# One-hot lanes of every other batch on ScalarE, Gelu's table loaded ahead, and four unread products on TensorE

## The chip, the cores and the metric

The kernel runs on one NeuronCore of a Trainium2 chip. The metric is the device time of one execution in microseconds (us), as the median of several runs. Before the change it is 1257.93 us (three runs, 1257.76 to 1258.65).

## The reference, cut to what matters

One layer of graph attention over 80,000 edges and 2,500 nodes, then a mixture of eight experts of which each node uses two:

```
x = x + relu(segment_sum(alpha * h[src], dst))            # h = layernorm(x) W, 4 heads of 64
xn = layernorm(layernorm(x)) * gamma + beta
logits = xn @ Wr + br;  top_vals, top_idx = top_k(logits, 2);  w = softmax(top_vals)
y = sum over e of  (gelu(xn @ W1[e] + b1[e]) @ W2[e] + b2[e]) * w_full[:, e]
out = x + y
```

Here x is 2500 x 256, W1 is 8 x 256 x 512, W2 is 8 x 512 x 256, everything in float32.

## The kernel before

The program is written by hand, one instruction stream for each engine, tied by semaphores (`wait_ge`, `then_inc`). Each stream is executed in order. It has three stages.

**Edges (to about 950 us).** GpSimd gathers rows of `h` by 664 indirect DMAs (L528). TensorE multiplies them with one-hot matrices of the destination (L640), VectorE weighs and accumulates (L1188, L1101). ScalarE makes those one-hot matrices in float32: for each tile of 128 edges `Square(dst - iota)` (L822), eight tiles at a time, and then `Relu(1 - square)` over the eight (L827), which is 1 where the square is 0, and else 0.

**Routing (950 to 1013 us).** TensorE transposes the nodes and forms the router's logits (L673, L682). VectorE finds each node's two experts and its rank in each, all by short instructions that depend on one another (L1294 to L1363). The result is a position for each of 40 columns of pairs (20 blocks of nodes, twice). A position is split into a lane (its last 7 bits, `lane_i`, copied to bfloat16 as `lane_f`) and a column (`col_f`). To turn the table round, from "where does this pair go" to "which pair sits here", VectorE makes for four batches of ten columns of pairs a one-hot of the lane (`lane_oh`, L1368), a one-hot of the column (`col_eq`, L1370) and its products with the node's lane and with the pair's number (`col_oh`, L1373, L1374). TensorE multiplies the two, 40 products into one PSUM bank (L701). Each batch is given over by `table_in`, the last product gives `table_done`. VectorE then turns the sums into indices (L1389 to L1398), and `where_ready` lets GpSimd start.

**Experts (1013 us to the end).** The pairs, sorted by expert, fill 27 blocks of 256 slots. GpSimd fetches the nodes of a block by two indirect DMAs (L539), four blocks ahead. TensorE runs `slots_T` (four transposes, L715), `layer_1` (eight products of 256 columns, L727) and `layer_2` (eight products, L741), in the order slots_T(0), slots_T(1), layer_1(0), then for each block j layer_1(j+1), slots_T(j+2), layer_2(j). ScalarE applies Gelu (`hidden`, L911), VectorE picks W1 (L1403), scales the transposed nodes (L1411) and adds b2 (L1419), GpSimd scatters the results (L548). At the end the results are read back and combined with the weights (L1460, L1461).

`hidden` is the first place that needs Gelu's table, so ScalarE loads it there. `xn1` holds the normalised nodes, `ones` is a 128 x 128 matrix of ones, `bank[7]` is a PSUM bank that is free between the edges and layer_2 of block 1, `fm` is a 1 x 4 tile of the edges' stage that is no longer read.

Of the kernel before, what the change touches and what calls it, by code (L numbers as in the profile page):

```python
# [37 lines left out]
def gat_moe_kernel(nc, x, src, dst, gnn_w, a_src, a_dst, gamma, beta, wr, br, w1, b1, w2, b2, out):  # L38
    fp32, bf16, i32 = mybir.dt.float32, mybir.dt.bfloat16, mybir.dt.int32
    ALU = mybir.AluOpType  # L40
    ACT = mybir.ActivationFunctionType
    AX = mybir.AxisListType
    P = 128


    N, F = x.shape
    H, _, FO = gnn_w.shape
    HF = H * FO
    KF = F // P
# [22 lines left out]
    assert NT % BT == 0 and CHUNKS * P == E and RING % PH == 0 and H * PH == P  # L72
    MW = HF + H
    NE, _, HID = w1.shape
    FC = HID // P
    BS = 256
# [21 lines left out]
    with ctx:  # L98
        def sb(name, shape, dt=fp32):
            return ctx.enter_context(nc.sbuf_tensor(name, shape, dt))  # L100

        def sem(name):
            return ctx.enter_context(nc.semaphore(name))

        psum = ctx.enter_context(nc.psum_tensor("psum", [P, 8, 512], fp32))
        bank = [psum[:, i, :] for i in range(8)]
# [6 lines left out]
        def early(width, dt=fp32):  # L113

            a = ring_flat[:, used[0]:used[0] + width]
            used[0] += width
            return a if dt == fp32 else a.bitcast(dt)
# [29 lines left out]
        start = early(NB + 1)  # L147
# [31 lines left out]
        ones = sb("ones", [P, P])  # L179
        iota_f = sb("iota_f", [P, P])  # L180
# [21 lines left out]
        old, fm, fm1 = sb("old", [1, H]), sb("fm", [1, H]), sb("fm1", [1, H])  # L202
# [21 lines left out]
        late = early  # L224
        xn1 = late(NB * F).rearrange("p (b f) -> p b f", b=NB)
# [26 lines left out]
        PAIRS = TOP * NB  # L252
        pos_i, lane_i, col_i = (late(PAIRS, i32) for _ in range(3))
        lane_f = late(PAIRS // 2, bf16)
        col_f = late(PAIRS)
        pair_f = late(PAIRS)
        iota_b = late(P // 2, bf16)
        CH = 10
# [6 lines left out]
        def over_x(width):  # L265
# [16 lines left out]
        lane_oh = shared[:, 0:PAIRS * P // 2].bitcast(bf16).rearrange("p (i n) -> p i n", i=PAIRS)  # L282
# [43 lines left out]
        SETS = ((0, 4), (4, 12), (12, NB))  # L326
        assert NB % 2 == 0 and NB % OUT_SET == 0 and SETS[-1][0] < NB - 1
        x_again_in = [sem(f"x_again_in{n}") for n in range(len(SETS))]
        z_stored, table_in, table_done, where_ready = (
            sem(n) for n in ("z_stored", "table_in", "table_done", "where_ready"))  # L330
        xT1_done, xT1_copied, logits_done = (
# [233 lines left out]
        def _(pe):  # L565
# [82 lines left out]
            for n, w in enumerate((wr_g, wr_b)):  # L648
                for k in range(KF):
                    last = pe.matmul(bank[7][:, n * NE:(n + 1) * NE], ones[:, :], w[:, k, :],  # L650
                                     start=(k == 0), stop=(k == KF - 1))
# [3 lines left out]
            for f in range(NPH - 1):  # L655
                n = f * PB
# [10 lines left out]
            def nodes_T(i):  # L667
                pe.wait_ge(x1_made, 1 + sum(2 * i + 2 > hi for _, hi in SETS))
                if i >= 2:
                    pe.wait_ge(xT1_copied, i - 1)  # L670
                for b in range(2):
                    for k in range(KF):
                        last = pe.transpose(bank[i % 2][:, (k * 2 + b) * P:(k * 2 + b + 1) * P],  # L673
                                            acc[:, 2 * i + b, k * P:(k + 1) * P], ident[:, :])
                last.then_inc(xT1_done, 1)
# [22 lines left out]
            for i in range(PAIRS):  # L698
                if i % CH == 0:
                    pe.wait_ge(table_in, i // CH + 1)  # L700
                last = pe.matmul(bank[5][:, 0:2 * NH], lane_oh[:, i, :],  # L701
                                 col_oh[:, i, :, :].rearrange("p s c -> p (s c)"),
                                 start=(i == 0), stop=(i == PAIRS - 1))
            last.then_inc(table_done, 1)

            def slots_T(j):
                u = j % 2
# [50 lines left out]
        def _(act):  # L760
# [94 lines left out]
            for f in range(NPH - 2):  # L855
                n = f * PB
# [6 lines left out]
            last = (NPH - 1) * PB  # L863
# [36 lines left out]

            act.wait_ge(gap_ready, 1)
            act.activation(w_b, tmp1, ACT.Exp).then_inc(gap_exp, 1)

            def hidden(j, u, first=False):
                e = act.value_load(blk_e[0:1, bass.ds(j, 1)], min_val=0, max_val=NE - 1)
                if not first:
                    act.wait_ge(l2_done, j - 1)
                for c in range(FC):
                    if c % 2 == 0:
                        act.wait_ge(l1_done, FC // 2 * j + c // 2 + 1)  # L910
                    act.activation(hT[:, u, c, :],  # L911
                                   bank[2 + 2 * u + c // 2][:, c % 2 * BS:(c % 2 + 1) * BS], ACT.Gelu,
                                   bias=b1_T[:, bass.ds(e * FC + c, 1)]).then_inc(gelu_done, 1)
# [24 lines left out]
        def _(v):  # L938
# [119 lines left out]
            for g in range(TG):  # L1058
                last = v.tensor_scalar(D_f[:, g, :], lay_d[:, g, :], d_sub[:, g:g + 1], None, ALU.subtract)
# [150 lines left out]
            for f in range(NPH - 1):  # L1210
                n = f * PB
# [18 lines left out]
            last = (NPH - 1) * PB  # L1230
# [125 lines left out]
            c.link(v.tensor_copy(pos_i, col_f))  # L1356
            c.link(v.tensor_scalar(lane_i, pos_i, P - 1, None, ALU.bitwise_and))
            c.link(v.tensor_copy(lane_f, lane_i))
            c.link(v.tensor_scalar(col_i, pos_i, 7, None, ALU.arith_shift_right))
            c.link(v.tensor_copy(col_f, col_i))  # L1360
            of_node = col_f.rearrange("p (k b) -> p k b", k=TOP)
# [3 lines left out]

            for n in range(PAIRS // CH):
                of = slice(n * CH, (n + 1) * CH)
                v.tensor_tensor(lane_oh[:, of, :], iota_b.unsqueeze(1).broadcast_to([P, CH, P]),  # L1368
                                lane_f[:, of].unsqueeze(2).broadcast_to([P, CH, P]), ALU.is_equal)
                c.link(v.tensor_tensor(col_eq[:, n % 2, :, :],  # L1370
                                       iota_f[:, 1:1 + NH].unsqueeze(1).broadcast_to([P, CH, NH]),
                                       col_f[:, of].unsqueeze(2).broadcast_to([P, CH, NH]), ALU.is_equal))
                c.link(v.tensor_scalar(col_oh[:, of, 0, :], col_eq[:, n % 2, :, :], pcol[:, 0:1], None, ALU.mult))  # L1373
                v.tensor_tensor(col_oh[:, of, 1, :], col_eq[:, n % 2, :, :],  # L1374
                                pair_f[:, of].unsqueeze(2).broadcast_to([P, CH, NH]), ALU.mult)\
                 .then_inc(table_in, 1)
                v.wait_ge(table_in, n + 1)
# [76 lines left out]
            for b in range(NB):  # L1454
                row = x1[:, b, :]
                if b % OUT_SET == 0:
                    n, times = b // OUT_SET, 2 if b + OUT_SET == NB else 1
# [29 lines left out]
```

## Time and profile before

| what | value |
|---|---|
| median of three runs | 1257.93 us |
| the profiled execution | 1254.97 us |
| its span on the core | 1253.2 us |
| TensorE busy with matmuls | 660.4 us (53%) |
| VectorE busy | 729.4 us (58%) |
| ScalarE busy | 410.8 us (33%) |
| GpSimd busy | 785.5 us (63%) |
| mean granted clock of TensorE | 0.759 of full speed |

The shares are means over stages with different limits, so the stretch around the change has to be read by itself. In a row of the profile L701 is line 701 of the kernel; PE is TensorE's products, PEld its weight loads, DVE is VectorE, ACT ScalarE, POOL GpSimd, SP the engine that only issues DMAs. The tiles `ring`, `RS_all` and `shared` are large buffers that many later tiles share, so they stand in the rows for `lane_oh` (shared), `col_oh` (RS_all) and most others (ring). PEclk is the clock granted to TensorE: 1.00 is 2.4 GHz, 0.50 is 1.2 GHz, and a value between them is a mean over a stretch that holds both.

### The profile page before, as it was taken

To read this page: it belongs to the slowest core of one execution; us is meant where nothing else is said; L and a number is where in the kernel's file an instruction comes from. 1 tells how busy PE (TensorE), PEld (TensorE's weight loads), DVE (VectorE), ACT (ScalarE), POOL (GpSimd) and SP (SyncE) were. 2 spreads that over 40 slices of the span, in tenths; PEclk is the share of its full clock that TensorE was granted. 3 is DMA by queue.
4 is the path that set the end of the run, shared out by engine and by line. 5 is a ranking of instruction groups with operands and counts; after the bars stand their busy time and mean duration, and the time that the engine had idled before them with its cause. 6 is when DMAs were issued, how large, how long until landed. Compare 5 with 4: busy or idle time off the path is not lost.

```text
span 1253.2 us, 10981 instructions
## 1 busy us (share of the span) xinstructions
PE 660.4 (53%) x2658; PEld 526.1 (42%) x2658; DVE 729.4 (58%) x1782; ACT 410.8 (33%) x1035; POOL 785.5 (63%) x835
## 2 busy tenths in 40 slices
PE   0530343355435643465435643366447459999990
PEld 0520232244223432244223432244336448888880
DVE  6711476558665676557665686557778843333325
ACT  3550243144322443144422443234521412222210
POOL 5577777777777777777777777777700025555540
PEclk9975667786678766777667776777777569999995
DMA  8464434444444434444344443444490212222217
GB/s 282 171 122 109 109 107 110 109 111 109 107 109 111 109 106 109 109 111 110 106 110 109 111 109 107 110 110 107 137 364 9 84 33 68 72 76 72 68 59 254
DMA packets 79451, 143.95 MB, mean 115 GB/s; under 512 B 22337, under 2 KB 50467, under 8 KB 79267
## 3 DMA queue, kind: packets, MB, share of 16 engines
q0 software_dynamic: 39664, 110.31, 31.7%
q1 hardware_dynamic: 37147, 30.44, 8.0%
q10 hardware_dynamic: 2584, 2.56, 0.6%
q8 instruction: 22, 0.36, 0.1%
q14 instruction: 34, 0.28, 0.1%
HBM read 126.48 MB, written 17.40 MB: 115 GB/s over the span
## 4 chain that ended last, share of the span: by engine, by line
POOL 50%; PE 19%; issue 18%; DVE 6%; DMA 2%; PEld 1%; ACT 1%; PEldq 1%; DVEq 0%; POOLq 0%
POOL ring L528 48%; PE psum L727 8%; PE psum L741 7%; PE psum L591 1%; POOL ring L500 1%; PEld psum L640 1%; PE psum L715 1%; PEldq L642 1%; PE psum L682 1%; DVE acc L1460 1%; DVE acc L1461 1%; PE psum L673 1%; ACT ring L878 1%; DMA ring<-in_dst,ring 1%; DMA h_tab<-ring 0%
## 5 line engine op out<-in xcount | busy, mean ns | idle before, releaser
L528 POOL DMA_INDIRECT ring<-h_tab,srcP x664 | 630.9, 950 | 204.4 <-issue 202.0
L640 PE MATMUL psum<-ring,shared 128*128 128x260 f32 x1328 | 389.2, 450 | 446.5 <-DVE acc L1101 388.4
L640 PEld LDWEIGHTS psum<-ring,shared 128*128 128x128 f32 x1328 | 285.9, 224 | 536.6 <-DVE acc L1101 403.9
L822 ACT ACTIVATE shared<-iota_f,Dcol 128x128 f32<-128x128 f32 x664 | 202.0, 386 | 33.2 <-PEq L642 33.2
L1188 DVE TENSOR_TENSOR ring<-ring,psum 128x2048 f32<-128x2048 f32 x83 | 189.8, 2287 | 2.8
L1101 DVE TENSOR_TENSOR acc<-acc,psum 128x260 f32 x332 | 140.0, 422 | 61.0 <-PEq L642 24.8
L840 ACT ACTIVATE Ex<-Z 128x128 f32<-128x128 f32 x21 | 6.5, 309 | 513.0 <-DVE Z L1155 513.0
L1123 DVE STREAM_TRANSPOSE TB<-ring 128x128 f32<-128x128 f32 x21 | 8.5, 403 | 222.8 <-DMA ring<-h_tab,srcP 222.8
L539 POOL DMA_INDIRECT ring<-z_tab,ring x54 | 52.5, 972 | 117.5 <-DVEq L1399 101.3
L548 POOL DMA_INDIRECT ys_tab<-shared,ring x54 | 54.3, 1005 | 87.6 <-DVE shared L1419 79.3
L727 PE MATMUL psum<-ring 128*128 128x256 f32 x432 | 99.5, 385 | 0.0
L741 PE MATMUL psum<-ring,RS_all 128*128 x432 | 97.5, 379 | 0.0
L827 ACT ACTIVATE shared<-shared,ones 128x1024 f32<-128x1024 f32 x83 | 95.3, 1149 | 2.7
L911 ACT ACTIVATE RS_all<-psum,tail_consts 128x256 f32<-128x256 f32 x108 | 45.1, 470 | 143.5 <-PE psum L727 143.5
L727 PEld LDWEIGHTS psum<-ring 128*128 128x128 f32 x432 | 83.5, 194 | 11.7
L741 PEld LDWEIGHTS psum<-ring,RS_all 128*128 128x128 f32 x432 | 80.1, 190 | 9.9
L1419 DVE TENSOR_TENSOR shared<-psum,links 128x512 f32<-128x512 f32 x27 | 18.7, 692 | 74.5 <-PE psum L741 74.5
L1411 DVE TENSOR_SCALAR ring<-psum,tail_consts 128x256 f32<-128x256 f32 x54 | 26.9, 539 | 53.4 <-PE psum L715 53.4
L1403 DVE COPY ring<-ring 128x1024 f32 x27 | 19.3, 715 | 15.5 <-issue 10.2
L515 POOL DMA_INDIRECT ed_tab<-e_node,spos x20 | 19.9, 993 | 13.3 <-ACT e_node L804 8.5
L500 POOL DMA_INDIRECT ring<-in_dst,ring x20 | 19.0, 949 | 10.5 <-issue 5.8
L715 PE MATMUL psum<-ident,ring 128*128 128x128 f32 x108 | 17.2, 284 | 8.2 <-DMA ring<-z_tab,ring 8.2
(287 smaller groups left out, 610.5 us busy)
## 6 DMA issues: line engine op xcount, KB each, us to landing
ring<-h_tab,srcP POOLq DMA_INDIRECT x664, 2.8
ring<-in_L_ffn_W SPq DMA_DIRECT2D x16, 512.0 KB, 11.5
h_tab<-ring SPq DMA_DIRECT2D x10, 260.0 KB, 2.5
ring<-in_x SPq DMA_DIRECT2D x1, 2432.0 KB
z_tab<-ring SPq DMA_DIRECT2D x2, 1024.0 KB, 4.4
ring<-ys_tab SPq DMA_DIRECT2D x4, 512.0 KB, 9.0
ring<-ys_tab ACTq DMA_DIRECT2D x4, 512.0 KB, 9.6
out<-acc SPq DMA_DIRECT2D x4, 512.0 KB
```

Of the source, the lines that this page charges most:

```text
L500: pool.indirect_dma_start(out=drow[:, b, :], out_offset=None, in_=dst_rows, in_offset=bass.IndirectOffsetOnAxis(ap=qi[:, b:b + 1], axis=0) ...
L528: pool.indirect_dma_start(out=ring[:, t % RING, :], out_offset=None, in_=h_tab, in_offset=bass.IndirectOffsetOnAxis(ap=srcP[:, t:t + 1], a ...
L539: pool.indirect_dma_start(out=xs_in[:, u, m, :], out_offset=None, in_=z_tab, in_offset=bass.IndirectOffsetOnAxis(ap=node_ix[:, BM * j + m: ...
L548: pool.indirect_dma_start(out=ys_tab, out_offset=bass.IndirectOffsetOnAxis(ap=dest_ix[:, BM * j + m:BM * j + m + 1], axis=0), in_=y_out[:, ...
L640: pe.matmul(sums[G_at % NSUM][:, 0:MW], dst_oh[:, n % OHB, 2 * g + r, :], ring[:, t % RING, :], start=(r == 0), stop=(r == 1))
L727: last = pe.matmul(bank[2 + 2 * u + c // 2][:, c % 2 * BS:(c % 2 + 1) * BS], w1_now[:, u, k, c * P:(c + 1) * P], xsT[:, u, k, :], start=(k ...
L741: last = pe.matmul(bank[6 + u][:, m * F:(m + 1) * F], hT[:, u, c, m * P:(m + 1) * P], w2_all[:, bass.ds(e, 1), c, :].rearrange("p e f -> p ...
L822: last = act.activation(dst_oh[:, n % OHB, k, :], iota_f[:, :], ACT.Square, scale=-1.0, bias=Dcol[:, t:t + 1])
L827: act.activation(batch, batch, ACT.Relu, scale=-1.0, bias=ones[:, 0:1]).then_inc(oh_made, 1)
L911: act.activation(hT[:, u, c, :], bank[2 + 2 * u + c // 2][:, c % 2 * BS:(c % 2 + 1) * BS], ACT.Gelu, bias=b1_T[:, bass.ds(e * FC + c, 1)]) ...
L1101: v.tensor_tensor(a, a, sums[(n * GB + g) % NSUM][:, 0:MW], ALU.add).then_inc(flushed, 1)
L1188: v.tensor_tensor(msg, msg, ex.unsqueeze(3).broadcast_to([P, BT, H, FO]), ALU.mult)
```

## The change

Batches 1 and 3 of `lane_oh` are made by ScalarE, in the manner of L822 and L827, with a bfloat16 result. For that VectorE writes a float32 copy of the lanes (`lane32`), unlinked, and signals `lanes_known`. TensorE waits for `lanes_made` beside `table_in` in those batches. After its one-hots ScalarE runs one Gelu over the 1 x 4 tile `fm`, whose result nobody reads. TensorE runs four products of 512 columns into `bank[7]` after the last product of L701; nobody reads them and they wait for nothing.

```diff
             for i in range(PAIRS):
                 if i % CH == 0:
                     pe.wait_ge(table_in, i // CH + 1)
+                    if i // CH % 2:
+                        pe.wait_ge(lanes_made, i // CH // 2 + 1)
...
             last.then_inc(table_done, 1)
+            for _ in range(4):
+                pe.matmul(bank[7], ones[:, :], xn1.rearrange("p b f -> p (b f)")[:, 0:512], start=True, stop=True)
...
             act.activation(w_b, tmp1, ACT.Exp).then_inc(gap_exp, 1)
+            act.wait_ge(lanes_known, 1)
+            for n in range(1, PAIRS // CH, 2):
+                for i in range(n * CH, (n + 1) * CH):
+                    last = act.activation(lane_oh[:, i, :], iota_f[:, :], ACT.Square, scale=-1.0,
+                                          bias=lane32[:, i:i + 1])
+                last.then_inc(lane_squared, 1)
+                act.wait_ge(lane_squared, n // 2 + 1)
+                of = lane_oh[:, n * CH:(n + 1) * CH, :].rearrange("p i n -> p (i n)")
+                act.activation(of, of, ACT.Relu, scale=-1.0, bias=ones[:, 0:1]).then_inc(lanes_made, 1)
+
+            act.activation(fm[:, :], fm[:, :], ACT.Gelu)
...
             c.link(v.tensor_copy(lane_f, lane_i))
+            v.tensor_copy(lane32, lane_i).then_inc(lanes_known, 1)
...
             for n in range(PAIRS // CH):
                 of = slice(n * CH, (n + 1) * CH)
-                v.tensor_tensor(lane_oh[:, of, :], iota_b.unsqueeze(1).broadcast_to([P, CH, P]),
-                                lane_f[:, of].unsqueeze(2).broadcast_to([P, CH, P]), ALU.is_equal)
+                if n % 2 == 0:
+                    v.tensor_tensor(lane_oh[:, of, :], iota_b.unsqueeze(1).broadcast_to([P, CH, P]),
+                                    lane_f[:, of].unsqueeze(2).broadcast_to([P, CH, P]), ALU.is_equal)
```

## Rows read from the trace of the kernel before

**Rows 1.** The chain that ended last: start us, length us, what (lengths are to its next piece).

```profile
996.18 1.49 DVE shared L1368
...
999.49 1.49 DVE shared L1368
...
1008.67 0.73 DVE RS_all L1374
1009.45 1.10 PE psum L701 x10
...
1013.16 0.94 POOL ring L539
...
1017.01 2.77 DMA ring<-z_tab,ring
...
1019.82 1.12 PE psum L715 x4
1020.94 8.87 PE psum L727 x32
```

**Rows 2.** The same chain later: one whole layer, and the last block's end.

```profile
1048.39 3.45 PE psum L727 x16
...
1213.45 3.47 PE psum L741 x16
```

**Rows 3.** Timeline of VectorE: start us, us, engine, line, operation, out<-in, count.

```profile
995.29 0.18 DVE L1358 CAST ring<-ring 128x40 bf16<-128x40 int32 x1
...
997.59 0.71 DVE L1370 TENSOR_TENSOR ring<-iota_f,ring 128x540 bf16<-128x540 f32 x1
...
1012.54 0.19 DVE L1397 CAST ring<-ring 128x54 int32<-128x54 f32 x1
1012.65 0.18 DVE L1398 CAST ring<-ring 128x54 int32<-128x54 f32 x1
```

**Rows 4.** Timeline of ScalarE in the edges' stage.

```profile
933.19 0.31 ACT L840 ACTIVATE Ex<-Z 128x128 f32<-128x128 f32 x1 [22.42 <-DVE Z L1155]
...
933.55 2.43 ACT L822 ACTIVATE shared<-iota_f,Dcol 128x128 f32<-128x128 f32 x8
936.01 1.15 ACT L827 ACTIVATE shared<-shared,ones 128x1024 f32<-128x1024 f32 x1
937.07 2.44 ACT L822 ACTIVATE shared<-iota_f,Dcol 128x128 f32<-128x128 f32 x8
```

**Rows 5.** The costliest groups: busy us, mean ns of one, idle before.

```profile
L822 ACT ACTIVATE shared<-iota_f,Dcol 128x128 f32<-128x128 f32 x664 | 202.0, 386 | 33.2 <-PEq L642 33.2
```

**Rows 6.** Timeline of ScalarE and TensorE around the first two expert blocks.

```profile
1017.36 1.09 PE L715 MATMUL psum<-ident,ring 128*128 128x128 f32 x4 [6.83 <-DMA ring<-z_tab,ring]
...
1024.47 1.28 ACT L911 ACT_TABLE_LOAD   x1 [35.54 <-PE psum L727]
1025.77 1.57 ACT L911 ACTIVATE RS_all<-psum,tail_consts 128x256 f32<-128x256 f32 x4
...
1029.64 0.60 PE L715 MATMUL psum<-ident,ring 128*128 128x128 f32 x4
```

**Rows 7.** Stretches: PE, PEld, DVE, ACT, POOL busy (instructions), PEclk, DMA share, GB/s.

```profile
1021.00:1024.50 3.50, 3.50 (x9) 2.77 (x9) 0.97 (x2) 0.03 (x1) 1.65 (x2) 0.50 0.38 112
1024.00:1025.00 1.00, 1.00 (x4) 0.79 (x4) 0.00 (x0) 0.53 (x1) 0.00 (x0) 0.61 0.15 57
```

**Rows 8.** The same for five earlier stretches, by which the clock's behaviour is read.

```profile
293.00:301.00 8.00, 7.77 (x18) 5.78 (x19) 7.18 (x11) 7.46 (x19) 5.93 (x7) 0.50 0.39 108
877.70:882.00 4.30, 0.00 (x0) 0.00 (x0) 0.00 (x0) 0.00 (x0) 3.09 (x4) 0.93 0.39 107
950.50:954.00 3.50, 0.00 (x0) 0.00 (x0) 2.97 (x7) 0.00 (x0) 0.00 (x0) 0.87 0.00 0
911.00:917.00 6.00, 5.40 (x17) 4.01 (x18) 5.15 (x9) 0.00 (x0) 0.82 (x1) 0.72 1.04 343
955.00:978.00 23.00, 21.05 (x101) 20.73 (x102) 21.34 (x54) 8.91 (x17) 0.00 (x0) 0.50 0.03 8
```

More of the change, by code:

```diff
@@ L254, in gat_moe_kernel @@
         lane_f = late(PAIRS // 2, bf16)
-        col_f = late(PAIRS)
+        col_f, lane32 = late(PAIRS), late(PAIRS)
         pair_f = late(PAIRS)
@@ L328, in gat_moe_kernel @@
         x_again_in = [sem(f"x_again_in{n}") for n in range(len(SETS))]
+        lanes_known, lane_squared, lanes_made = (sem(n) for n in ("lanes_known", "lane_squared", "lanes_made"))
         z_stored, table_in, table_done, where_ready = (
```

## The prediction

> **What bounds the kernel now.** I read the chain of waits first, because the shares of busy time (no engine is over 63%) are means over three stages that have nothing in common. Around the change the chain has one engine at a time [rows 1]. From 996.18 to 1009.40 it is VectorE alone, four rounds of one-hots, 3.31 us each (999.49 less 996.18). Then come the ten products of the last batch (1.10 us from 1009.45), the indices on VectorE, and GpSimd, whose fourth fetch is issued at 1015.76 and lands 2.77 us after 1017.01. The transposes of slots_T(1) wait for it and start at 1019.82. From 1020.94 TensorE never stops: 8.87 us for the first two layer_1, and then 3.45 us for every layer to the end of the last block at 1216.92 [rows 1, 2]. Behind that block stands a serial tail (scatter, read-back, combination). So whatever lets layer_1(0) start earlier, or makes it shorter, should move the end by as much.
>
> The second thing to see is the clock. Two layers should take 2 x 3.45 = 6.90 us and took 8.87. From 1021.0 to 1024.5 the granted clock was 0.50, which is 1.2 GHz, and the stretch from 1024 to 1025 has a mean of 0.61, so it rose at about 1024.8, 3.84 us after the first wide product [rows 1, 7]. Running 3.84 us at half speed costs 1.92 us, which is nearly the whole difference of 1.97.
>
> **Part 1: the lanes.** Each batch that VectorE no longer makes saves the spacing between L1368 and the next instruction, 997.59 less 996.18, thus 1.41 us and not the 1.49 of its duration, as the two overlap [rows 1, 3]. Two batches: 2.82 us. The unlinked copy lane32 costs the spacing that two such casts have when only the second is waited for: 1012.65 less 1012.54, 0.11 us [rows 3]. All four rounds were on the chain, so the net is 2.71 us. The rounds then end at 999.60, 1001.50, 1004.81 and 1006.71, and the last ten products start at 1006.74, against 1009.45.
>
> This holds if ScalarE keeps up. lanes_known comes a cast after lane_f, at about 995.7 (the cast before it starts at 995.29, with a spacing of 0.22) [rows 3]. Eight Squares take 936.01 less 933.55, 2.46 us, so 0.31 each, and ten take 3.08. A Relu over 1024 elements takes 937.07 less 936.01, 1.06 us, and for 1280 about 1.33. One batch is 4.4 us: lanes_made comes at 1000.2 and 1004.6, and is wanted at 1001.5 and 1006.7 [rows 4]. By the full duration of 386 ns for each Square, with no overlap, and 1.15 x 1.25 = 1.44 for a Relu, it comes at 1001.0 and 1006.3, still in time [rows 4, 5]. No table is loaded in between: Exp, Square and Relu follow each other without one [rows 4]. No row shows ScalarE writing bfloat16. I bound it by nothing and by twice the time of these rows, and take nothing, as the width and the function are those of rows 4. So the cover is 1.3 to 2.1 us; below that every microsecond of delay comes off the gain. Queued behind the new waits on ScalarE is only `hidden`, which has nothing to do before the first layer_1. TensorE's added wait is for a signal that is already there; I cost it at 0 to 0.1 us, and take 0.
>
> The page ScalarE: Activation LUTs of the Trainium skill (Rules for kernel authors) speaks against this part: it says to use VectorE and not ScalarE for relu and simple arithmetic, as VectorE is faster for each element. This case's rows agree on the durations (4.4 us against 1.41 for a batch), but the rule would only give another sum if ScalarE were on the chain.
>
> **Part 2: Gelu's table.** The load takes 1.28 us at 1024.47, and the first four Gelus end at 1027.34 [rows 6]. layer_2(0) is the first to want them, and it stands behind layer_1(1) and slots_T(2), which end at about 1030.2 [rows 1, 6]. The load is hidden now with 2.9 us to spare, so loading it earlier is worth 0. After the change it lies behind ScalarE's last Relu, from 1004.6 to about 1006.1, when nothing waits for ScalarE. DVE's and POOL's queues don't see it. If all of layer_1 ran at 2.4 GHz, the spare would still be over 1 us.
>
> **Part 3: the four products.** They have 4 x 512 columns, as many as one layer_1 (8 x 256): 3.45 us at 2.4 GHz and 6.9 at 1.2 [rows 2]. They start when the last batch's products end, at about 1007.84 (1006.74 + 1.10), and would end at 1014.7 if the clock stayed low. The slots of block 0, which came at 1017.36, come at 1014.65 now, and those of block 1 at 1017.11 [rows 1, 6]. So even the worst case delays slots_T(0) by 0.1 us, and that has over 1 us to spare before slots_T(1). In themselves they cost nothing; the question is what they do to the clock.
>
> From the one rise that follows dense work without a gap, 3.84 us after its start, I expect it at about 1011.7 [rows 1, 7]. Then (6.9 - 3.84) / 2 = 1.53 us of work is left, and the products end at about 1013.2. From there to layer_1(0), at about 1017.7 (1017.11 and a transposition of 0.60), TensorE has only eight transposes. That is a gap of 4.5 us. In the trace the clock fell from 1.00 after 2.6 us (950.5 to 954.0, mean 0.87: 0.13 / 0.5 x 3.5 = 0.9 us at half) and after 3.7 us (877.7 to 882.0, mean 0.93) of an idle TensorE [rows 8]. So it most likely falls again, between 1015.8 and 1017.7. Whether transposes hold it up isn't clear from that. From 955 to 978, when TensorE was busy 21.05 of 23 us with transposes and products of 8 columns, the clock stayed at 0.50 [rows 8], so they do not raise it.
>
> The page TensorE: Matmul & The Clock Gate of the Trainium skill (Part 4: PE-mode transpose) says that transposes don't count as activity of TensorE for its clock. The row from 955 to 978 agrees. By this rule the fall is likelier, and the sum would be nearer to 2.71 us than to 5.15.
>
> If it falls there, layer_1(0) starts at half speed as before. The stretch from 911 to 917 (mean 0.72, so 0.28 / 0.5 x 6 = 3.4 us at half) has a fall followed by a rise as soon as work was dense [rows 8]. With 3.4 us at half instead of 3.84, the layers gain 0.2 us. The transposes of slots_T(1), 1.12 us at half and 0.60 at full, gain up to 0.52 if the fall comes behind them [rows 1, 6]. I take 0.5 us. The bounds: at best the clock stays up, and 1.97 + 0.52 = 2.5 us are gained. At worst it has just fallen, and the half-speed stretch is longer than now. The longest of the trace is at least 8.0 us of mostly dense work (293 to 301, mean 0.50) [rows 8], and by it (8.0 - 3.84) / 2 = 2.1 us would be lost.
>
> **The sum.** 2.71 + 0 + 0.5 = 3.2 us. The profiled execution took 1254.97 us, 1253.2 of it in the span; it would take 1251.8. It is 3 us below the median of the timed runs, so I take the difference to the median: 1257.93 - 3.2 = 1254.7 us.
>
> **The rivals.**
>
> *The clock is held.* The gap of 4.5 us turns out short enough, with transposes in it, that the clock stays up to layer_1(0). For it: it once stayed up 3.7 us without any work [rows 8]. Against it: the gap is longer than both idle stretches before a fall. The gain is 2.71 + 2.5 = 5.2 us, 1252.7 us.
>
> *The clock is raised and falls too early.* It rises late in the products, falls at about 1015, and a new rise comes only after 5.5 us of layer_1 instead of 3.84. For it: the longer half-speed stretch at 293. Against it: 3.84 and 3.4 us are as common. It costs 0.8 us, the gain is 1.9 us, 1256.0 us.
>
> *ScalarE becomes the bound (slower than before).* A Square with a bfloat16 result takes twice as long as rows 4 have it. Its 22 instructions must fit in the 11.0 us from 995.7 to 1006.7; from there the gain shrinks, and from 13.75 us (0.31 becoming about 0.49 a Square) the kernel is slower than before. At twice the time, 17.6 us, the last products start at 1013.3, 3.9 us later than now, and the fetches with them: 1261.8 us. Against it: the durations of rows 4 in the same form but for the output's width.
>
> *The earlier start is not passed on.* GpSimd or the weights for the first blocks would have to end last. Against it: the chain is on TensorE alone behind 1020.94 [rows 1]. 1257.9 us.
>
> **How the numbers follow.** The forecast gets 0.50, the clock held 0.20, the early fall 0.20, ScalarE 0.05, nothing passed on 0.05. A measurement of this kernel can tell about 0.2% from no change, 2.5 us. The forecast is over that by 0.7 us, so I give 0.45 of its 0.50 to faster. With the clock held (0.20) and a little of the early fall (0.04) faster has 0.69. Same has 0.05 + 0.16 + 0.05 = 0.26, and slower 0.05. The range takes in the two rivals of the clock and a few tenths beyond: 1252.3 to 1257.1 us.
>
> **What would show it.** L1368 has two instructions instead of four, the first product of the last batch starts 2.7 us earlier relative to L1358, and VectorE has no wait for ScalarE. lanes_made comes before table_in in both batches: no idle time of TensorE before L701 is put down to ScalarE. The table load stands behind ScalarE's 22 one-hot instructions, and the time to the end falls by nothing for it. The granted clock rises inside the four products and has a second stretch at 0.50 that begins before layer_1(0). The first two layers take between 6.9 us (clock held) and over 9. The prediction is wrong if the last batch's products wait for ScalarE, if slots_T(0) waits for the four products by more than 1 us, or if the clock doesn't rise in them at all.

## The result and the profile after

The changed kernel takes 1252.92 us (median of 7 runs, 1251.29 to 1254.50), against 1257.93 us before (7 runs, 1257.10 to 1259.99). The ratio is 0.9959, 95% interval 0.9949 to 0.9969: 5.0 us less. The forecast was 1254.7.

The chain that ended last, after (start us, us, what); its lines answer to [rows 1]:

```profile
997.47 1.49 DVE shared L1387
...
1000.78 0.73 DVE ring L1389
...
1002.69 1.49 DVE shared L1387
...
1007.93 1.10 PE psum L704 x10
...
1011.64 0.94 POOL ring L540
...
1015.49 2.70 DMA ring<-z_tab,ring
...
1018.23 0.66 PE psum L719 x4
1018.89 6.91 PE psum L731 x32
```

VectorE now makes two batches of lanes; the batch after each goes straight to L1389. The two layers take 6.91 us instead of 8.87, and the transposes ahead of them 0.66 instead of 1.12.

The two executions are best compared from the same instruction, the cast that makes `lane_f` (995.29 before, 996.49 after). From it, the last batch's products start after 14.16 us before and 11.44 after; layer_1(0) starts after 25.65 and 22.40; the first two layers end after 34.52 and 29.31. That is 5.21 us: 2.72 in the lanes, 0.07 in the fetches, 0.46 in the transposes, 1.96 in the layers. What follows is as long as before: 223.4 us to the end of the span before (1253.2 less 1029.81) and 223.3 after (1249.1 less 1025.80). The cast after:

```profile
996.49 0.18 DVE L1375 CAST ring<-ring 128x40 bf16<-128x40 int32 x1
```

The profiled execution itself is only 3.7 us under that of before (1251.29 against 1254.97): its cast comes 1.2 us later, and 0.4 us more of it lies outside the span. The later cast comes from a place ahead of every edited instruction. In the edges' last batches TensorE ran at 1.2 GHz for longer, and sixteen products (L640 before, L641 after) took 6.81 us instead of 5.16. Their stretch (PE, PEld, DVE, ACT, POOL busy, PEclk, DMA share, GB/s), before:

```profile
936.61 5.16 PE L640 MATMUL psum<-ring,shared 128*128 128x260 f32 x16 [2.07 <-DVE ring L1189]
...
936.60:942.40 5.80, 5.56 (x18) 4.34 (x19) 3.34 (x6) 4.05 (x10) 0.00 (x0) 0.75 0.72 268
```

and after:

```profile
936.16 6.81 PE L641 MATMUL psum<-ring,shared 128*128 128x260 f32 x16 [2.06 <-DVE ring L1206]
...
936.10:942.40 6.30, 6.24 (x15) 4.91 (x16) 2.96 (x6) 4.10 (x10) 0.00 (x0) 0.50 0.70 257
```

ScalarE and TensorE after, in the timeline:

```profile
996.93 3.03 ACT L912 ACTIVATE shared<-iota_f,ring 128x128 bf16<-128x128 f32 x10 [6.78 <-DVE ring L1376]
...
999.99 1.36 ACT L917 ACTIVATE shared<-shared,ones 128x1280 bf16<-128x1280 bf16 x1
...
1004.31 1.36 ACT L917 ACTIVATE shared<-shared,ones 128x1280 bf16<-128x1280 bf16 x1
...
1005.69 1.28 ACT L919 ACT_TABLE_LOAD   x1
...
1008.81 6.26 PE L710 MATMUL psum<-ring,ones 128*128 128x512 f32 x8
```

ScalarE ends batch 1 at 1001.35 and batch 3 at 1005.67; TensorE takes them up at 1002.71 and 1007.93, and both times waited for VectorE last. And the clock, in stretches after:

```profile
1008.80:1014.00 5.20, 5.20 (x9) 2.16 (x7) 3.48 (x13) 0.00 (x0) 1.99 (x2) 0.50 0.09 25
1014.00:1015.00 1.00, 1.00 (x3) 0.19 (x1) 0.00 (x0) 0.00 (x0) 0.76 (x1) 0.99 0.33 90
1015.10:1018.80 3.70, 1.20 (x9) 0.99 (x10) 0.99 (x2) 0.00 (x0) 2.79 (x4) 1.00 0.35 100
1019.00:1025.00 6.00, 6.00 (x30) 5.28 (x29) 1.61 (x3) 2.46 (x6) 1.89 (x2) 1.00 0.24 66
```

It rose 5.2 us into the four products and was still up when layer_1(0) began 3.8 us after their end.

### The profile page after: what moved, and what is told of

The parts are those of the page before. It is cut to its first block, busy times and chain, and to the rows that moved or that the text cites. A ratio compares the mean times of both kernels' runs of the same rounds, so it can differ in the third digit from the quotient of the medians.

```text
span 1249.1 us, 11021 instructions
## 1 busy us (share of the span) xinstructions
PE 661.5 (53%) x2666; PEld 524.6 (42%) x2666; DVE 726.1 (58%) x1781; ACT 419.7 (34%) x1058; POOL 784.9 (63%) x835
## 3 DMA queue, kind: packets, MB, share of 16 engines
q0 software_dynamic: 39664, 110.31, 31.9%
## 4 chain that ended last, share of the span: by engine, by line
POOL 50%; PE 19%; issue 18%; DVE 6%; DMA 2%; PEld 1%; ACT 1%; PEldq 1%; DVEq 0%; POOLq 0%
POOL ring L529 49%; PE psum L731 7%; PE psum L745 7%; PE psum L592 1%; POOL ring L501 1%; PEld psum L641 1%; PEldq L643 1%; PE psum L719 1%; PE psum L683 1%; DVE acc L1479 1%; DVE acc L1480 1%; ACT ring L882 1%; PE psum L674 1%; DMA ring<-in_dst,ring 1%; DMA h_tab<-ring 1%
## 5 line engine op out<-in xcount | busy, mean ns | idle before, releaser
L529 POOL DMA_INDIRECT ring<-h_tab,srcP x664 | 630.8, 950 | 204.6 <-issue 201.9
L641 PE MATMUL psum<-ring,shared 128*128 128x260 f32 x1328 | 387.0, 448 | 450.5 <-DVE acc L1118 391.9
L641 PEld LDWEIGHTS psum<-ring,shared 128*128 128x128 f32 x1328 | 284.1, 222 | 540.2 <-DVE acc L1118 407.4
L592 PE MATMUL psum<-ring 128*128 128x264 f32 x80 | 20.3, 398 | 0.0
```

The source lines that it names most:

```text
L529: pool.indirect_dma_start(out=ring[:, t % RING, :], out_offset=None, in_=h_tab, in_offset=bass.IndirectOffsetOnAxis(ap=srcP[:, t:t + 1], a ...
L592: last = pe.matmul(bank[2 + 2 * (i % 2) + b][:, 0:wide], xT0[:, i % 2, b, k, :], w_ext[:, k, :], start=(k == 0), stop=(k == KF - 1))
L641: pe.matmul(sums[G_at % NSUM][:, 0:MW], dst_oh[:, n % OHB, 2 * g + r, :], ring[:, t % RING, :], start=(r == 0), stop=(r == 1))
```

## The experiments

They ran on three other chips, where the kernel before takes 1397.68 us (e1 to e4), 1399.06 (e5 to e8) and 1392.33 (e9 to e12). The 140 us more lie in the edges' stage: the cast comes at 1133 to 1143 us there. The runs of one kernel scatter by 5 to 9 us and the 95% interval of a ratio is 3 to 5 us wide, about what is to be told apart, so each kernel is read by its profile too. A profile is one execution, and it shows one course of the clock. "To the layers' end" is the time from the cast to the end of the first two layer_1, 34.5 us before and 29.3 after (the cast's start is read to 0.1 us).

**e1, the lanes alone.** Without the early Gelu and the products.

```diff
-            for _ in range(4):
-                pe.matmul(bank[7], ones[:, :], xn1...[:, 0:512], start=True, stop=True)
...
-            act.activation(fm[:, :], fm[:, :], ACT.Gelu)
```

> The change without the early Gelu and without the four products. Theory (lanes and clock add up): the last batch's products start 2.7 us earlier after the lane cast than before, the first two layer_1 still take 8 to 9.5 us because they begin at 1.2 GHz, and the median is 2.5 to 3.2 us under before, about 1255.2. Rival (the whole 5 us comes from the lanes, the clock is chance): about 1253 us.

Measured: 1396.72 us, ratio 0.9988 (0.9977 to 0.9999), so 0.1 to 3.2 us under before. Timeline of TensorE, and the stretch in which its clock rose:

```profile
1154.51 1.08 PE L704 MATMUL psum<-RS_all,shared 128*128 128x108 bf16 x10 [0.83 <-DVE RS_all L1390]
...
1165.73 9.54 PE L729 MATMUL psum<-ring 128*128 128x256 f32 x32
```
```profile
1170.00:1171.00 1.00, 1.00 (x4) 0.86 (x3) 0.00 (x0) 0.99 (x2) 0.00 (x0) 0.64 0.00 0
```

The last products start 11.4 us after the cast, as forecast: the 2.7 us are there. The layers begin at 1.2 GHz and the clock rises 4.8 us into them (3.84 before), so they cost 0.5 us more than in the profile of before. To the layers' end 32.2 us, 2.3 under before. The interval holds that, though the medians differ by only 1.0 us where the theory had 2.5 to 3.2; the rival's 5 us are excluded.

**e2, the products alone.** The kernel before with the loop of four products of the change.

```diff
             last.then_inc(table_done, 1)
+            for _ in range(4):
+                pe.matmul(bank[7], ones[:, :], xn1...[:, 0:512], start=True, stop=True)
```

> The kernel before with the four unread products alone. Theory: VectorE's rounds stay at 3.31 us each; the clock rises inside the products, holds, and the first two layer_1 take 6.9 us: 1.5 to 2.5 us under before, about 1255.7. Rival (the clock is chance, the products do nothing): 1257.9, and the first two layer_1 at 8 us or more.

Measured: 1394.81 us, ratio 0.9979 (0.9968 to 0.9990). TensorE's timeline:

```profile
1151.15 6.01 PE L706 MATMUL psum<-ring,ones 128*128 128x512 f32 x8
...
1161.09 7.07 PE L729 MATMUL psum<-ring 128*128 128x256 f32 x32
```

The layers take 6.9 us. To their end 32.0 us, 2.5 under before. So both parts work alone. Their 2.3 and 2.5 us add up to 4.8, and the 0.4 that are missing to the 5.2 of the whole are the layers of e1, which were 0.5 us slower than those of before.

**e3, no early Gelu.**

```diff
-            act.activation(fm[:, :], fm[:, :], ACT.Gelu)
```

> The changed kernel without the early Gelu. Theory: the table is loaded at the first Gelu of the experts, 1.3 us hidden behind layer_1(1), and the time is that of the changed kernel, 1252.9 within 0.7. Rival (with both layers at 2.4 GHz the load is no longer hidden): layer_2(0) starts up to 1.3 us later behind slots_T(2), 1254.2.

Measured: 1392.65 us, ratio 0.9969 (0.9956 to 0.9982), the same ratio as the changed kernel in e5. ScalarE's timeline:

```profile
1164.54 1.28 ACT L927 ACT_TABLE_LOAD   x1 [15.04 <-issue]
...
1168.02 0.84 ACT L927 ACTIVATE RS_all<-psum,tail_consts 128x256 f32<-128x256 f32 x2 [0.24 <-PE psum L731]
1169.74 0.84 ACT L927 ACTIVATE RS_all<-psum,tail_consts 128x256 f32<-128x256 f32 x2 [0.87 <-PE psum L731]
```

The load stands between the first products and the first Gelus and by 1168.02 ScalarE waits for TensorE again. To the layers' end 29.3 us, and layer_2(0) follows without a gap at 1170.04. So the chain gains nothing by the early Gelu. The time within 0.7 us of the changed kernel wasn't tested, as that kernel wasn't run on this chip.

**e4, transposes for products.**

```diff
-            for _ in range(4):
-                pe.matmul(bank[7], ones[:, :], xn1...[:, 0:512], start=True, stop=True)
+            for n in range(24):
+                pe.transpose(bank[7][:, n % 4 * P:(n % 4 + 1) * P], xn1[:, n % 4, 0:P], ident[:, :])
```

> The changed kernel with 24 unread transposes of 128 columns (about 6.5 us at 1.2 GHz) in the place of the four wide products. Theory (only wide products raise the clock): it stays at 0.50 to the layers, which take 8 to 9.5 us, and the time is that of the lanes alone, about 1255.2. Rival (any busy TensorE will do): the clock rises and the time is 1252.9.

Measured: 1396.28 us, ratio 0.9992 (0.9979 to 1.0004). TensorE's clock in stretches:

```profile
1148.40:1151.50 3.10, 3.10 (x18) 3.10 (x16) 2.04 (x11) 0.00 (x0) 0.26 (x1) 0.50 0.00 0
1152.00:1153.00 1.00, 0.92 (x9) 0.68 (x7) 0.98 (x2) 0.00 (x0) 0.70 (x2) 1.00 0.12 20
...
1156.00:1158.90 2.90, 1.58 (x8) 1.19 (x7) 0.99 (x2) 0.00 (x0) 1.99 (x4) 0.50 0.33 96
```

My theory fell: the clock rose in the 24 transposes, 3.5 us after the first. They then ran faster and ended at 1152.9, and 2.4 idle us later, just before slots_T(0), it was down. The layers took 8.58 us, and it is 31.4 us to their end. So the time is near that of the lanes alone, for another reason than I gave.

**e5, the changed kernel again.** No edit.

> The changed kernel once more, on the chip of this call, as the mark for the other three. Theory (lanes 2.7 us, clock held 2.0 to 2.9 us by the four products and the transposes behind them): 4.5 to 5.5 us under before, first two layer_1 in 6.9 us, last batch's products 11.4 us after the lane cast. Rival (the clock was held in two profiles by luck and often falls in the gap): first two layer_1 at 8 us or more, about 3 us under before.

Measured: 1395.03 us, ratio 0.9969 (0.9956 to 0.9982), by which it is 4.3 us under before, 2.5 to 6.2 by the interval (the medians differ by 4.0).

```profile
1154.00:1155.00 1.00, 1.00 (x3) 0.43 (x3) 0.98 (x2) 0.00 (x0) 0.72 (x1) 0.90 0.32 82
1156.00:1160.20 4.20, 1.20 (x9) 0.99 (x10) 1.00 (x2) 0.00 (x0) 3.29 (x4) 1.00 0.40 114
```

Here the clock rose at 1154.2, 4.0 us into the products, and they ended at 1155.8, so 4.5 us before layer_1(0). It stayed up all the same. To the layers' end 29.3 us.

**e6, two products.**

```diff
-            for _ in range(4):
+            for _ in range(2):
```

> The changed kernel with two unread products instead of four. They last 3.45 us at 1.2 GHz and leave 3.6 us of idle TensorE before slots_T(0). Theory (work must last until the clock is up, and the gap behind it must be short): the clock rises at their end or not at all, has fallen by layer_1(0), and the time is 1.5 to 2.7 us over the changed kernel. Rival (any push is enough): equal to the changed kernel.

Measured: 1397.43 us, ratio 0.9990 (0.9979 to 1.0001), 2.4 us over e5.

```profile
1155.00:1157.00 2.00, 0.84 (x1) 0.00 (x0) 1.35 (x2) 0.00 (x0) 1.69 (x2) 0.71 0.19 53
1157.00:1159.00 2.00, 0.00 (x0) 0.00 (x0) 0.10 (x1) 0.00 (x0) 1.39 (x3) 1.00 0.25 78
1160.00:1162.00 2.00, 0.45 (x2) 0.45 (x3) 0.87 (x2) 0.00 (x0) 1.67 (x2) 0.50 0.35 102
```

The clock rose 0.3 us behind the products' end (1155.8), was up over idle time, and was down again before slots_T(1): 31.7 us to the layers' end. Here a push that ended with the rise was wasted.

**e7, six products.**

```diff
-            for _ in range(4):
+            for _ in range(6):
```

> The changed kernel with six unread products. With a rise 5 us after their start they end 7.7 us after it, 0.7 us after the slots of block 0 land, and before those of block 1. Theory: slots_T(0) starts 0.5 to 1 us later, layer_1(0) as before, both layers in 6.9 us, time equal to the changed kernel within 0.7 us; the clock is held more safely. Rival (the delay of slots_T(0) is passed on): up to 1 us over the changed kernel.

Measured: 1394.76 us, ratio 0.9964 (0.9947 to 0.9981), as e5.

```profile
1152.65 7.90 PE L710 MATMUL psum<-ring,ones 128*128 128x512 f32 x12
1160.39 0.60 PE L719 MATMUL psum<-ident,ring 128*128 128x128 f32 x4
...
1162.61 7.07 PE L731 MATMUL psum<-ring 128*128 128x256 f32 x32
```

slots_T(0) starts 0.7 us later behind the products, and nothing comes of it: 29.4 us to the layers' end.

**e8, the clock raised before the table.** `unread(n)` issues n products of 512 columns into `bank[7]`. They read `acc`, which TensorE already waited for.

```diff
+            unread(7)
             for i in range(PAIRS):
+                if i == 2 * CH:
+                    unread(1)
...
-            for _ in range(4):
-                pe.matmul(bank[7], ones[:, :], xn1...[:, 0:512], start=True, stop=True)
+            unread(6)
```

> The changed kernel with seven unread products of 512 columns (of acc, which is ready by then) ahead of the table's first batch, one before its third batch, and six instead of four behind its last. Theory: TensorE runs at 2.4 GHz from the table's batches on, the last ten products take 0.6 instead of 1.1 us, the six end before the slots of block 0 land, and the clock holds to the layers: 0.5 us under the changed kernel. Rival (the extra products stand in the way of the table's batches or the clock falls between them): equal or up to 1 us over it.

Measured: 1394.62 us, ratio 0.9973 (0.9960 to 0.9985), equal to e5 within the scatter.

```profile
1149.05 0.66 PE L711 MATMUL psum<-RS_all,shared 128*128 128x108 bf16 x10 [1.25 <-DVE RS_all L1399]
...
1159.07 0.66 PE L725 MATMUL psum<-ident,ring 128*128 128x128 f32 x4 [1.76 <-DMA ring<-z_tab,ring]
```

The last ten products take 0.66 us instead of 1.08, and GpSimd starts 14.9 us after the cast instead of 15.2; 29.0 us to the layers' end, 0.3 under e5. The timing can't tell that. The clock did not stay up as the theory had it: it fell 5.7 us after the cast, so the second ten products took 1.08 us, and it was up again 9.1 us after the cast.

**e9, three batches by ScalarE.**

```diff
-                    if i // CH % 2:
-                        pe.wait_ge(lanes_made, i // CH // 2 + 1)
+                    if i // CH:
+                        pe.wait_ge(lanes_made, i // CH)
...
-            for n in range(1, PAIRS // CH, 2):
+            for n in range(1, PAIRS // CH):
...
-                if n % 2 == 0:
+                if n == 0:
                     v.tensor_tensor(lane_oh[:, of, :], ...
```

> The changed kernel with batches 1, 2 and 3 of the lanes by ScalarE. Theory (the lanes are free only while ScalarE is ahead): three batches of 4.35 us from 0.4 us after the lane cast end at 13.5 us, so the last batch's products start there and not at 11.4, put down to ScalarE: 2.1 us over the changed kernel, 2.8 us under before. Rival (VectorE alone sets the pace): they start at 10.0 us and the kernel is 1.4 us under the changed one.

Measured: 1391.71 us, ratio 0.9989 (0.9978 to 1.0000). TensorE's timeline and its clock:

```profile
1147.44 1.06 PE L704 MATMUL psum<-RS_all,shared 128*128 128x108 bf16 x10 [3.25 <-ACT shared L917]
```
```profile
1157.00:1158.00 1.00, 0.28 (x2) 0.28 (x3) 0.00 (x0) 0.00 (x0) 0.69 (x2) 0.55 0.23 66
```

The last batch's products start 13.6 us after the cast and wait for ScalarE, 2.2 us later than in e5. The other thing is new: with the same four products the clock rose only 2.0 us into them, and fell again at 1157.1, 4.2 us after their end and 1.7 us before layer_1(0). The layers took 7.80 us. To their end 32.8 us, 1.7 under before where the theory had 2.8.

**e10, ten products.**

```diff
-            for _ in range(4):
+            for _ in range(10):
```

> The changed kernel with ten unread products, which don't fit ahead of the slots. Theory (products cost nothing only while they end before slots_T(1)): with a rise 4 to 5.2 us after their start they end 10.6 to 11.2 us after it, 1.2 to 1.8 us after the slots of block 1 land; both transposes and VectorE's copy of block 0 come behind them, and layer_1(0) starts 1.8 to 3 us later than in the changed kernel, which is 1.8 to 3 us over it. Rival (the fetches or the copies end last anyway): within 0.7 us of the changed kernel.

Measured: 1390.79 us, ratio 0.9987 (0.9977 to 0.9997), so 0.4 to 3.2 us under before.

```profile
1145.05 10.89 PE L710 MATMUL psum<-ring,ones 128*128 128x512 f32 x20
1155.77 1.04 PE L719 MATMUL psum<-ident,ring 128*128 128x128 f32 x8
1157.46 7.17 PE L731 MATMUL psum<-ring 128*128 128x256 f32 x32 [0.65 <-DVE ring L1430]
```

Both transposes queue behind the products, layer_1(0) waits for the copy behind them, and starts 2.3 us later than in e5; 31.9 us to the layers' end. The products end 23.2 us after the cast, and in e5 the transposes of block 1 begin at 21.8: past the slots' arrival the products cost time.

**e11, a version meant to beat both.** e8 with two further edits.

```diff
-                for i in range(n * CH, (n + 1) * CH):
+                width = 3 if n == 2 else CH
+                for i in range(n * CH, n * CH + width):
...
             slots_T(0)
+            layer_1(0, range(0, FC // 2))
             slots_T(1)
-            layer_1(0)
+            layer_1(0, range(FC // 2, FC))
```

> A version meant to beat both: the early unread products of the run before this call, three of the ten lanes of batch 2 by ScalarE too, and slots_T(1) put between the halves of layer_1(0), so that the layer starts when the slots of block 0 are copied. Theory: last batch's products 0.4 us earlier (11.0 after the lane cast), first half of layer_1(0) about 21.0, both layers over 28.2 us after the cast, against 29.3 in the changed kernel and 34.5 before: about 6.1 us under before. Rival (ScalarE is late with batch 3, or layer_1(1) waits for the copy of block 1): 29 us, equal to the changed kernel.

Measured: 1387.56 us, ratio 0.9965 (0.9953 to 0.9976). TensorE's timeline and its clock:

```profile
1151.01 0.63 PE L725 MATMUL psum<-ident,ring 128*128 128x128 f32 x4 [1.79 <-DMA ring<-z_tab,ring]
1152.72 3.38 PE L737 MATMUL psum<-ring 128*128 128x256 f32 x8 [1.09 <-DVE ring L1440]
```
```profile
1152.00:1153.00 1.00, 0.28 (x1) 0.28 (x2) 0.67 (x2) 0.00 (x0) 0.81 (x1) 0.58 0.46 131
```

The three lanes bring 0.4 us (last products 11.05 us after the cast), and layer_1(0) starts at 20.4 instead of 22.4. But the clock fell at 1152.2, half a microsecond before, and the first half of the layer ran at 1.2 GHz: 29.4 us to the layers' end, no less than in e5. No version was shown to beat the changed kernel.

**e12, narrow products.** One execution, for its profile.

```diff
-            for _ in range(4):
-                pe.matmul(bank[7], ones[:, :], xn1...[:, 0:512], start=True, stop=True)
+            for _ in range(18):
+                pe.matmul(bank[7][:, 0:NE], ones[:, :], xn1[:, 0, 0:NE], start=True, stop=True)
```

> The changed kernel with 18 unread products of 8 columns (about 6.8 us at 1.2 GHz) in the place of the four of 512. Theory (TensorE busy with narrow products doesn't raise the clock, transposes and wide ones do): the clock stays at 0.50 until 3.5 to 6 us into layer_1(0), and both layers take 8 to 10 us. Rival (being busy is enough): the clock rises within them as it did with 24 transposes.

```profile
1145.30:1152.90 7.60, 7.60 (x39) 7.60 (x37) 3.47 (x13) 0.00 (x0) 3.86 (x4) 0.50 0.17 50
1153.00:1160.00 7.00, 6.33 (x20) 5.09 (x21) 1.99 (x4) 0.59 (x2) 3.79 (x4) 0.51 0.33 94
```

TensorE was busy for 7.6 us without a break and the clock stayed at 1.2 GHz, to about 4 us into the layers, which took 8.92 us. The rival is excluded: in the same place, behind the same 20 products of the table, the clock rose in 24 transposes (e4) and in four products of 512 columns (e5), but not in 18 products of 8 columns.

## Why the prediction was right, and where it was not

**The lanes: right.** 2.71 us forecast, 2.72 measured. Ten Squares took 3.03 us (3.08 forecast) and the Relu 1.36 (1.33), both with a bfloat16 result, so the bound of twice the time went unused. e9 shows the rival's mechanism where it is real: a third batch puts ScalarE on the chain.

**Gelu's table: right**, by e3. **The four products as such: right.** They fit ahead of the slots; with six (e7) nothing was lost yet, with ten (e10) 2.3 us were.

**The clock: the term was mis-sized.** I put 0.5 us on it, and it was worth 2.42 (0.46 in the transposes, 1.96 in the layers), nearly its upper bound of 2.5. The step that failed is "So it most likely falls again, between 1015.8 and 1017.7". Two readings went into it. The first was the rise, taken from a single row as 3.84 us after the start. It came after 5.2, 4.7, 5.2 and 4.0 us in the four profiles with four products right behind VectorE's last batch (after, e2, e3, e5). Each microsecond of delay makes the products end half a microsecond later and the gap shorter: the rise came 1.2 us earlier after the cast in e5 than in the changed kernel, and the products ended 0.6 us earlier. But this reading alone doesn't explain the miss. In e5 the rise and the gap of 4.5 us were as forecast, and the clock was held all the same. So it is the second reading that failed as a rule, that the clock falls in a gap of this length though transposes are in it. It rested on two falls in an idle TensorE (2.8 and 3.8 us after the last product, 2.6 and 3.7 as the prediction counts them from the starts of its stretches) and on the row of 955 to 978 [rows 8], from which I read that transposes count for nothing. That stretch mixes them with products of 8 columns:

```profile
963.10 1.09 PE L673 MATMUL psum<-ident,acc 128*128 128x128 f32 x4
963.99 1.71 PE L682 MATMUL psum<-tail_consts,ring 128*128 128x8 f32 x8
```

e4 and e12 take the two apart: the clock rose in transposes alone, and did not in narrow products. The page TensorE: Matmul & The Clock Gate of the Trainium skill (Part 4: PE-mode transpose), which says that transposes don't count, is contradicted by e4 for the float32 transposes of this kernel, and the measurement decides. So the eight transposes in the gap may have helped to hold the clock; no run took them away, and this stays argued.

The rival "the clock is held" was the right case, with 1252.7 us (its terms are 2.71 and 2.5; the 5.15 us beside the page is the same case, added up less closely). But it isn't certain to be held. Of nine profiles with four products or more it was up to the layers in seven (after, e2, e3, e5, e7, e8, e10; in e7 and e10 there was next to no gap to bridge) and fell in two. The length of the gap alone doesn't decide: it held over 4.5 us in e5, and fell 2.9 us after the products in e11. What decides was not settled.

**The way to the median.** 5.21 us in one pair of profiles and 5.0 in the medians agree, though the two whole profiled executions differ by 3.7. On another chip the changed kernel gained 2.5 to 6.2 us (e5).

## What to carry to other kernels

Work that nobody reads can pay where an engine idles ahead of dense work. Here it had to run past the rise of the clock (e6), end before the data arrived (e10) and leave little idle time behind, and even then the clock was not held every time (e9, e11). When a stretch at low clock is to be explained, separate the kinds of work in it before calling one of them without effect. And a single duration of an effect that starts at no fixed point of the program is one draw, not its size: look at several in the trace before it goes into a sum.

## What was not expected of the hardware

The same kernel takes 1257.93 us on one chip and 1392 to 1399 on three others. After the lane cast the stages agree to 0.1 us where the clock took the same course (e3 and e5 with the changed kernel); the difference is in the gathers. GpSimd's idle time ahead of L528 (us, times), before, on the first chip ("issue" is time in which the profile shows nothing that it waits for, PEq is TensorE's sequencer):

```profile
  issue: 202.0, 663
```

and ahead of the same line (L529) in e5:

```profile
  issue: 192.7, 622
  PEq L643: 123.0, 42
```

In e5 GpSimd waits 123 us for TensorE to finish its batches, and in the other runs on those chips 118 to 127 us. TensorE itself stands still ahead of its products of that stage (L640 or L641) for 406 to 448 us in those runs with no cause in the profile, against 55.3 before and 55.8 after on the first chip. What holds TensorE up there was not tried.
